# Second layer by single batches, expert rows added on TensorE, whole rows scattered to their experts

## The chip, the cores and the metric

The kernel runs on one core of one Trainium2 chip. The metric is the device time in microseconds (us) of one execution. TensorE is PE below, VectorE DVE, ScalarE ACT, GpSimd POOL, SyncE SP.

## What is computed

Two transformer layers over x, 8 batches of 128 rows of 256 numbers (1024 tokens). Each layer is cross-attention and then a mixture of experts. The change lies in the second layer, of which this is the reference:

```python
def _L1_xattn_ref(q, k, v):
    scale = 1.0 / jnp.sqrt(jnp.asarray(dk, dtype=q.dtype))
    scaled = jnp.einsum('bsd,bse->bde', q, k) * scale
    attn = jax.nn.softmax(scaled, axis=1)
    return jnp.einsum('bde,bse->bsd', attn, v)
...
def _L1_ffn_ref(x, router_w, expert_bias, gate_proj, up_proj, down_proj):   # 16 experts, 4 chosen, inner width 224
    logits = jnp.einsum('bsh,eh->bse', x, router_w) + expert_bias
    scores = jax.nn.softmax(logits, axis=-1)
    top_w, top_idx = jax.lax.top_k(scores, TOP_K)
    top_w = top_w / jnp.sum(top_w, axis=-1, keepdims=True)
    g = jnp.einsum('bsh,khe->bske', x, gate_proj)
    u = jnp.einsum('bsh,khe->bske', x, up_proj)
    out = jnp.einsum('bske,keh->bskh', jax.nn.silu(g) * u, down_proj)
    sel = jnp.take_along_axis(out, top_idx[..., None], axis=2)
    return jnp.sum(sel * top_w[..., None], axis=2)
...
x = x + _L0_xattn_ref(...)
x = x + _L0_ffn_ref(_layernorm(x), ...)          # 64 experts, 8 chosen
x = x + _L1_xattn_ref(_layernorm(x), ctx, ctx)
x = x + _L1_ffn_ref(_layernorm(x), ...)
```

## The kernel before

The program is a row of phases with a barrier of all engines between them. The first layer (projection, attention, experts) ends at about 449 us. The second layer is three phases.

**Features phase** (`features_phase`). SP loads, for each batch, the eight weighted expert rows of every token from the first layer (`ft_g_rows`, 1 MB a batch). The batches go in three groups, (0, 1), (2, 3, 4), (5, 6, 7). For a group DVE adds the eight rows and x (`Combine.dve_sum`), takes mean and variance, computes the inverse root with three Newton steps for the whole group (`Norm`), and writes the normalised rows. PE makes the scores (two matmuls of 128 by 256 a batch), DVE their maximum, ACT the exponentials and the scaled values, PE the sum over values (`ft_ps_out`, two matmuls of the same shape), DVE adds it to x. Then DVE normalises again (`Routing.dve_normalise`), PE turns the rows and multiplies by the gate. DVE's choice of the four experts (`dve_choose`) and the places in the lists (`dve_places`) of a group stand in the step of the next group. SP stores the normalised rows to `normed`; POOL scatters one number for each choice into a table, 32 indirect transfers in all. `Plan` turns the counts into a list of tiles, and then SP loads the weights of the first six tiles.

**Tiles phase** (`tiles_phase`). 42 tiles of at most 128 choices of one expert, in rounds of six buffers. For each tile POOL copies its column of the list (L1616), gathers the 128 rows from `normed` by an indirect transfer (L1620), and later scatters the result of the tile six before (L1625). PE turns the rows of the next tile, does the down matmuls of the tile two before, then the up matmuls of this one. SP loads a tile's weights, 448 and 224 KB, when the tile six before is through its down matmuls. The list has places for 128 choices in each tile; places that no choice fills gather some row and scatter it to spare rows.

**Last phase** (`last_phase`). SP loads four rows a token, DVE adds them with their weights to x, two batches interleaved, four operations each (L2045), ACT stores.

The first layer already routes one batch at a time with `RowRouting` and `Rstd`, and already scatters whole rows to their experts and clears the rows beyond. The order in all phases is written out by hand: each engine's block is a loop that issues in program order, and an instruction that waits holds all behind it on its engine or queue.

## Time and profile before

| | us |
|---|---|
| median of 3 runs (lowest, highest) | 775.46 (774.98, 780.38) |
| profiled execution, its own time | 776.06 |
| its span on the core | 774.3 |
| features phase, first rows there to the plan's end | 463.6 to 572.9 |
| tiles phase, first issue to last POOL issue | 593.2 to 742.7 |
| last phase to the span's end | 752.4 to 774.3 |

Share of the span busy: PE 62%, DVE 49%, POOL 44%, ACT 27%. The page gives the stages away by its clock row: the granted clock of TensorE is near full speed in the tiles and near half in the features phase. Times below are from the start of the span. The span and the execution's own time differ by 1.8 us, which lie around the span.

### The profile page before, as it was taken

To read this page: it belongs to the slowest core of one execution; us is meant where nothing else is said; L and a number is where in the kernel's file an instruction comes from. 1 tells how busy PE (TensorE), PEld (TensorE's weight loads), DVE (VectorE), ACT (ScalarE), POOL (GpSimd) and SP (SyncE) were. 2 spreads that over 40 slices of the span, in tenths; PEclk is the share of its full clock that TensorE was granted. 3 is DMA by queue.
4 is the path that set the end of the run, shared out by engine and by line. 5 is a ranking of instruction groups with operands and counts; after the bars stand their busy time and mean duration, and the time that the engine had idled before them with its cause. 6 is when DMAs were issued, how large, how long until landed. Compare 5 with 4: busy or idle time off the path is not lost. (4 is left out here: it accounts for less than half of the span.)

```text
span 774.3 us, 11100 instructions
## 1 busy us (share of the span) xinstructions
PE 477.6 (62%) x3303; PEld 360.8 (47%) x3303; DVE 380.1 (49%) x1226; ACT 207.7 (27%) x533; POOL 340.2 (44%) x464
## 2 busy tenths in 40 slices
PE   1715976887784209987899703254500889899920
PEld 1611533444442108876688602233400888888810
DVE  8955555888854503533344405878640123222217
ACT  0540453555563104322233201021100222222200
POOL 9483210555554533644455510030552566666510
PEclk9965897999977558999999955565655799999965
DMA  5199896764889638899954239100034499999716
GB/s 164 54 197 302 319 294 178 200 168 138 264 287 348 235 119 261 273 331 302 305 183 158 78 115 402 62 1 21 21 88 136 128 294 291 287 294 291 235 46 252
DMA packets 83086, 157.18 MB, mean 203 GB/s; under 512 B 12523, under 2 KB 53493, under 8 KB 81248
## 3 DMA queue, kind: packets, MB, share of 16 engines
q1 hardware_dynamic: 54928, 91.89, 37.7%
q10 hardware_dynamic: 14944, 32.71, 13.5%
q0 software_dynamic: 13168, 32.02, 12.4%
q8 instruction: 22, 0.36, 0.2%
q14 instruction: 24, 0.20, 0.1%
HBM read 102.95 MB, written 56.12 MB: 205 GB/s over the span
## 5 line engine op out<-in xcount | busy, mean ns | idle before, releaser
L1140 DVE TENSOR_REDUCE at_top<-at_ps_top 128x2 f32<-128x512 f32 x128 | 83.5, 685 | 50.7 <-PE at_ps_top L1051 49.7
L1514 POOL DMA_INDIRECT rows<-hd_out,hd_rows x64 | 62.2, 972 | 68.6 <-DVE hd_out L1465 45.9
L1367 PE MATMUL hd_ps_up<-hd_x_turned,e_arena 128*128 128x160 f32 x512 | 84.8, 310 | 0.0
L1213 ACT ACTIVATE at_prob<-at_ps_score 128x512 f32<-128x512 f32 x128 | 71.6, 593 | 44.8 <-PE at_ps_score L1069 44.3
L1672 PE MATMUL l_ps_up<-l_x_turned,e_up_w 128*112 128x128 f32 x672 | 82.8, 278 | 0.0
L1672 PEld LDWEIGHTS l_ps_up<-l_x_turned,e_up_w 128*112 128x112 f32 x672 | 81.6, 182 | 2.6
L1367 PEld LDWEIGHTS hd_ps_up<-hd_x_turned,e_arena 128*128 128x128 f32 x512 | 78.2, 197 | 8.9 <-issue 6.2
L845 POOL DMA_INDIRECT held<-e_extended,e_address x64 | 62.8, 980 | 34.3 <-issue 18.9
L642 POOL DMA_INDIRECT table<-choice,ft_r_address x32 | 30.6, 957 | 104.4 <-DVE ft_r_address L633 95.6
L1051 PE MATMUL at_ps_top<-e_arena 96*128 96x256 bf16 x256 | 57.0, 312 | 26.4 <-PEq L110 21.7
L1502 DVE TENSOR_TENSOR hd_inner<-hd_silu,hd_ps_up 128x160 f32<-128x160 f32 x64 | 20.5, 321 | 77.9 <-ACT hd_silu L1452 77.9
L1069 PE MATMUL at_ps_score<-e_arena 99*128 99x256 bf16 x256 | 52.1, 294 | 8.7 <-DMA e_arena<-at_top_rows 8.7
L1761 DVE TENSOR_TENSOR l_inner<-l_silu,l_ps_up 112x256 f32<-112x256 f32 x42 | 17.7, 421 | 79.6 <-ACT l_silu L1711 79.6
L1620 POOL DMA_INDIRECT l_rows<-normed,l_column x42 | 41.0, 976 | 33.1 <-POOL l_column L1616 33.1
L1625 POOL DMA_INDIRECT rows<-l_out,l_target x42 | 41.3, 983 | 18.2 <-issue 9.8
L1081 PE MATMUL at_ps_out<-at_prob,e_arena 128*32 128x256 f32 x512 | 44.5, 423 | 4.0 <-ACT at_out L1196 3.6
L1943 PE MATMUL ft_ps_scores<-ft_x_norm,ft_keys 128*128 128x256 f32 x32 | 14.6, 645 | 51.0 <-DVE ft_x_norm L161 51.0
L1051 PEld LDWEIGHTS at_ps_top<-e_arena 96*128 96x128 bf16 x256 | 23.8, 106 | 43.7 <-issue 23.6
L1654 PE MATMUL l_ps_out<-e_down_w,l_inner 112*128 112x256 f32 x168 | 43.3, 380 | 0.1
L1662 PE MATMUL l_ps_x<-identity,l_rows 128*128 128x128 f32 x84 | 18.1, 298 | 40.8 <-DMA l_rows<-normed,l_column 40.7
L1452 ACT ACTIVATE hd_silu<-hd_ps_up 128x160 f32<-128x160 f32 x64 | 19.5, 304 | 85.3 <-PE hd_ps_up L1367 85.3
L1465 DVE TENSOR_SCALAR hd_out<-hd_ps_out,hd_rows 128x256 f32<-128x256 f32 x64 | 31.0, 484 | 21.2 <-PE hd_ps_out L1373 19.4
(277 smaller groups left out, 867.3 us busy)
## 6 DMA issues: line engine op xcount, KB each, us to landing
e_up_w<-in_up SPq DMA_DIRECT2D x42, 448.0 KB, 4.5
held<-e_empty ACTq DMA_DIRECT2D x16, 960.0 KB, 6.9
e_arena<-in_weights ACTq DMA_DIRECT2D x32, 384.0 KB, 5.1
e_arena<-in_weights SPq DMA_DIRECT2D x32, 384.0 KB, 11.7
hd_rows<-held SPq DMA_DIRECT2D x15, 768.0 KB, 10.8
e_down_w<-in_down SPq DMA_DIRECT2D x42, 224.0 KB, 5.6
ft_g_rows<-rows SPq DMA_DIRECT2D x8, 1024.0 KB, 10.9
parts<-op_parts SPq DMA_DIRECT2D x8, 576.0 KB, 6.5
```

Source lines behind the costliest of these rows:

```text
L845: self.nc.gpsimd.indirect_dma_start(self.held_dram, to, self.held.extended[:, b, :], None).then_inc(self.held.scattered, 16)
L1051: last = nc.tensor.matmul(ps_top[at % TOPS][:, half, :], q_in[n][0:TOP, columns(at, half)], k_in[n][0:TOP, columns(at)], start=True, stop= ...
L1069: last = nc.tensor.matmul(ps_score[at % SCORES][:, half, :], k_in[n][0:ROWS, columns(at, half)], q_in[n][0:ROWS, columns(at)], start=True, ...
L1081: last = nc.tensor.matmul(ps_out[32 * j:32 * j + VW, g % 2, :], v_in[:, b, half, 4 * g + j, :], prob[(4 * group + j) % RING][:, half, :], ...
L1140: nc.vector.reduce_max(top[:, 2 * h:2 * h + 2], ps_top[at % TOPS][:], AX_X).then_inc(top_found, 1)
L1213: nc.scalar.activation(prob[at % RING][:], ps_score[at % SCORES][:], ACT.Exp, scale=scale).then_inc(prob_ready, 1)
L1367: op = nc.tensor.matmul(ps_up[e % 2][:, part, :], w[:, k, part * P:(part + 1) * P], x_turned[g % 2][:, j, k, :], start=k == 0, stop=k == 1)
L1514: nc.gpsimd.indirect_dma_start(rows_out, to, out_ap, None, bounds_check=TOKENS * LAYER0.chosen - 1, oob_is_err=False).then_inc(semaphore, 16)
L1620: nc.gpsimd.indirect_dma_start(rows[u][:], None, normed_dram, of).then_inc(gathered[u], 16)
L1625: nc.gpsimd.indirect_dma_start(rows_out, to, out[u][:], None).then_inc(stored[u], 16)
L1654: op = nc.tensor.matmul(ps_out[u % 2][:], inner[u % 2][:, c * P:(c + 1) * P], down_w[u][:, c, :], start=c == 0, stop=c == C - 1)
L1672: op = nc.tensor.matmul(ps_up[u % 2][:, part, c * P:(c + 1) * P], up_w[u][:, k, at:at + W], x_turned[u % 2][:, k, :], start=k == 0, stop=k ...
```

## The change

The second layer takes the first layer's scheme.

- Features by single batches, steps t = 0 to 9. DVE adds only the upper four expert rows to the lower four (`halve`). PE adds those four and x through the identity in one accumulation, `ps_x`, and the attention's sum goes into the same accumulation. The first inverse root moves to POOL (`pool_scale`: a power and two Newton steps), ACT applies both normalisations and copies x back to SBUF.
- Routing by `RowRouting`: the row, with the weights and targets of all experts behind it (288 numbers), is scattered to `listed`, which has 1024 places for each expert; 32 indirect transfers as before, of 1152 bytes a row. No `normed`, no table.
- Tiles: POOL clears the places of a tile that no row fills (an indirect transfer that leaves out the filled ones), SP waits for that and loads the tile as a plain block, then its weights. DVE picks the weight and the target by the expert's number and weights the result. Targets of empty places are out of bounds and are left out.
- Last phase: DVE adds by halves and to x, batch by batch.

```diff
 class Rstd:
+    def pool_scale(self, pool, link, b):
+        pool.wait_ge(self.known, b + 1)
+        link(nc.gpsimd.tensor_scalar(full, self.mean_var[:, 1:2], EPS, None, ALU.add))
+        link(nc.gpsimd.tensor_tensor(root, full, self.power[:], ALU.pow))
+        for _ in range(NEWTON - 1):
+            link(nc.gpsimd.tensor_tensor(square, root, root, ALU.mult))
+            link(nc.gpsimd.tensor_scalar(work, square, full, -0.5, ALU.mult, ALU.mult))
+            link(nc.gpsimd.tensor_scalar(root, work, 1.5, root, ALU.add, ALU.mult))
+        nc.gpsimd.tensor_scalar(shift, self.mean_var[:, 0:1], root, -1.0, ALU.mult, ALU.mult).then_inc(self.ready, 1)
...
 def features_phase
         @block.gpsimd
+            for t in STEPS:
+                if t < B:
+                    first.pool_scale(pool, link, t)
+                if t >= 2:
+                    for k in range(layer.chosen):
+                        routing.pool_scatter(pool, t - 2, k)
         @block.tensor
+            def add_rows(b):
+                pe.wait_ge(halved, b + 1)
+                if b >= 2:
+                    pe.wait_ge(x_kept, b - 1)
+                    pe.wait_ge(routing.normed, b - 1)
+                for k in range(HALF):
+                    nc.tensor.matmul(ps_x[b % 2][:], consts.identity[:], rows[b][:, k, :], start=k == 0, stop=False)
+                nc.tensor.matmul(ps_x[b % 2][:], consts.identity[:], x_all[:, b, :], start=False, stop=True).then_inc(summed, 1)
...
         @block.vector
+            routing.dve_start(link)
+            halve(0)
+            for t in STEPS:
+                if t < B:
+                    dve.wait_ge(summed, t + 1)
+                    first.dve_stats(dve, link, t, ps_x[t % 2][:])
+                if 1 <= t <= B:
+                    dve.wait_ge(attended, t)
+                    second.dve_stats(dve, link, t - 1, ps_x[(t - 1) % 2][:])
+                    second.dve_scale(dve, link, t - 1)
+                if t >= 2:
+                    routing.dve_targets(dve, link, t - 2)
+                    routing.dve_places(dve, link, t - 2)
+                if t < B:
+                    dve.wait_ge(scored, t + 1)
+                    link(nc.vector.reduce_max(top[:], ps_scores[t % 2][:], AX_X))
+                    nc.vector.tensor_scalar(minus_top[t % 2][:], top[:], -scale, None, ALU.mult).then_inc(top_known, 1)
+                if t + 1 < B:
+                    halve(t + 1)
+                if 1 <= t <= B:
+                    routing.dve_choose(dve, link, t - 1)
+                if t < B:
+                    dve.wait_ge(expo_ready, t + 1)
+                    nc.vector.reciprocal(share[t % 2][:], total[t % 2][:]).then_inc(share_ready, 1)
+                if t == B:
+                    plan.dve_plan(dve, link)
...
 def tiles_phase
         @block.sync
+            def load_rows(i, u):
+                c = sp.value_load(experts.tile_column[0:1, bass.ds(i * U + u, 1)], min_val=0, max_val=layer.columns)
+                sp.wait_ge(cleared[u], i * 16 + 16)
+                sp.dma_start(rows[u][:], by_tile[bass.ds(c, 1)].rearrange("a p n -> (a p) n")).then_inc(rows_loaded[u], 16)
...
                     sp.wait_ge(down_done, i * U + u - U + 1)
+                    load_rows(i, u)
                     experts.load(sp, i, u)
         @block.gpsimd
             with pool.Fori(1, last + 1) as i:
                 for u in range(U):
                     pool.wait_ge(out_kept, i * U + u - U + 1)
-                    gather(i, u)
+                    clear(i, u)
                     scatter(i - 1, u)
         @block.vector
+            def pick(i, u, free):
+                e = dve.value_load(experts.tile_expert[0:1, bass.ds(i * U + u, 1)], min_val=0, max_val=E - 1)
+                nc.vector.tensor_copy(weight[u][:], rows[u][:, bass.ds(e * 2 + D, 1)])
+                nc.vector.tensor_copy(target[u][:], rows[u].bitcast(I32)[:, bass.ds(e * 2 + (D + 1), 1)])
```

The order on PE in the features phase, around the second group, before (`ft_ps_out` is the attention's sum, `ft_r_ps_narrow` holds logits and ranks, an x4 or x6 is two matmuls for each batch of the group):

```order
L533 MATMUL ft_r_ps_turned<-identity,ft_r_norm 128x128 x4
L548 MATMUL ft_r_ps_narrow<-ft_gate,ft_r_turned_sb 128x16 x4
L1943 MATMUL ft_ps_scores<-ft_x_norm,ft_keys 128x256 x6
L613 MATMUL ft_r_ps_narrow<-l_mask,earlier 128x16 x2
L615 MATMUL ft_r_ps_narrow<-l_mask,ones 128x16
L1952 MATMUL ft_ps_out<-ft_expo,ft_vals_shared 128x256 x6
```

The same place now, step 2 (turn of batch 1, scores of batch 2, logits of batch 1, the adding of batch 3, rank of batch 1, attention's sum of batch 2):

```order
L593 MATMUL ft_ps_turned<-identity,e_extended 128x128 x2
L1728 MATMUL ft_ps_scores<-ft_x_norm,ft_keys 128x256 x2
L604 MATMUL ft_ps_logits<-ft_gate,ft_r_turned_sb 128x16 x2
L1718 MATMUL ft_ps_x<-ft_rows,identity 128x256 x4
L1719 MATMUL ft_ps_x<-x_all,identity 128x256
L637 MATMUL ft_ps_rank<-bases,ones 128x16
L639 MATMUL ft_ps_rank<-e_mask,ones 128x16
L641 MATMUL ft_ps_rank<-e_mask,earlier 128x16
L1734 MATMUL ft_ps_x<-ft_expo,ft_vals_shared 128x256 x2
```

Five matmuls of 128 by 256 now stand ahead of the attention's sum in each step, and the turn of one batch stands ahead of the scores of the next.

SP's queue in the tile loop, one tile, before:

```order
L447 TENSOR_LOAD l_tile_expert
L447 ISA x2
L449 ISA
L449 DMA e_up_w<-in_up 128x896
L449 ISA
L449 DMA e_down_w<-in_down 112x512
```

And now (`listed` is the DRAM table of whole rows; the wait for the clearing is ahead of L1429):

```order
L1427 TENSOR_LOAD e_tile_column
L1427 ISA x2
L1429 ISA
L1429 DMA l_rows<-listed 128x288
L413 REGISTER_ALU
L413 TENSOR_LOAD e_tile_expert
L413 ISA x2
L415 ISA
L415 DMA e_up_w<-in_up 128x896
L415 ISA
L415 DMA e_down_w<-in_down 112x512
```

The load of the rows came from POOL's queue to SP's, ahead of the same tile's weights and behind those of the tile before.

## Rows read from the trace of the kernel before

**Rows 1.** Windows by stage: length, busy PE, PEld, DVE, ACT, POOL; clock, DMA, GB/s.

```profile
463.60:572.90 109.30, 42.84 (x158) 31.66 (x158) 80.08 (x374) 16.84 (x59) 22.23 (x24) 0.56 0.25 93
...
600.70:742.70 142.00, 127.29 (x924) 117.09 (x924) 38.09 (x126) 31.61 (x85) 88.33 (x123) 0.97 0.81 251
```

**Rows 2.** Timeline, POOL in the tiles: start, length, engine, line, operation, [idle before].

```profile
651.62 0.20 POOL L1616 COPY l_column<-l_lists 128x2 int32 x1
652.60 0.97 POOL L1620 DMA_INDIRECT l_rows<-normed,l_column  x1 [0.79 <-POOL l_column L1616]
653.87 0.99 POOL L1625 DMA_INDIRECT rows<-l_out,l_target  x1 [0.30 <-issue]
...
655.85 0.99 POOL L1620 DMA_INDIRECT l_rows<-normed,l_column  x1 [0.79 <-POOL l_column L1616]
```

**Rows 3.** Timeline, DVE's copy of a result ahead of the first of these.

```profile
649.89 0.41 DVE L1755 COPY l_out<-l_ps_out 128x256 f32<-128x256 f32 x1
```

**Rows 4.** One tile's answer (l_rows): landing of its transfers from issue.

```profile
DMA to landing us min/median/max: 2.7/5.0/6.2
```

**Rows 5.** Timeline, end of the features phase and the first issue of the tiles.

```profile
572.61 0.28 DVE L1843 CAST l_tile_expert<-ft_r_ps_turned 1x128 int32<-1x128 f32 x1
...
582.78 0.33 SPq L449 DMA_DIRECT2D e_down_w<-in_down  x1
582.78 0.96 POOL L642 DMA_INDIRECT table<-choice,ft_r_address  x1 [0.31 <-issue]
593.22 0.33 SPq L1598 DMA_DIRECT2D l_choices<-table  x1
```

**Rows 6.** Timeline, PE in the features phase: two batches, then three.

```profile
473.80 3.75 PE L1943 MATMUL ft_ps_scores<-ft_x_norm,ft_keys 128*128 128x256 f32 x8 [32.62 <-DVE ft_x_norm L161]
...
535.18 5.49 PE L1943 MATMUL ft_ps_scores<-ft_x_norm,ft_keys 128*128 128x256 f32 x12 [8.78 <-DVE ft_x_norm L161]
```

**Rows 7.** Groups by form, DVE in the features phase.

```profile
L1875 DVE TENSOR_TENSOR ft_g_rows<-ft_g_rows 128x1024 f32<-128x1024 f32 x8 | 9.8, 1221 | 5.2 <-DMA ft_g_rows<-rows 5.2
...
L1995 DVE TENSOR_REDUCE ft_top<-ft_ps_scores 128x2 f32<-128x512 f32 x8 | 5.5, 692 | 7.7 <-PE ft_ps_scores L1943 7.7
L1875 DVE TENSOR_TENSOR ft_g_rows<-ft_g_rows 128x512 f32<-128x512 f32 x8 | 5.5, 692 | 0.3
...
L1875 DVE TENSOR_TENSOR ft_g_rows<-ft_g_rows 128x256 f32<-128x256 f32 x8 | 3.4, 425 | 0.3
```

**Rows 8.** Timeline, first layer, one batch: statistics, root, ACT, turn, mask.

```profile
244.63 0.43 DVE L729 BATCH_NORM_STATS2 at_n_stats<-x_all 128x6 f32<-128x256 f32 x1
...
247.28 0.60 ACT L772 ACTIVATE e_extended<-x_all,at_n_scale 128x256 f32<-128x256 f32 x1 [7.38 <-DVE at_n_scale L743]
...
247.94 0.69 PE L778 MATMUL at_ps_merge<-identity,e_extended 128*128 128x128 f32 x2 [3.87 <-ACT e_extended L772]
...
251.16 0.20 DVE L801 TENSOR_SCALAR e_mask<-at_r_taken 128x64 bf16<-128x64 f32 x1
```

**Rows 9.** Timeline, a chain of seven dependent small POOL operations, first and last.

```profile
88.01 0.25 POOL L1022 TENSOR_SCALAR at_top_cut<-at_top 128x16 bf16<-128x16 f32 x1 [9.24 <-DVE at_top L1140]
...
89.83 0.25 POOL L1028 TENSOR_SCALAR at_top_parts<-at_top_rest 128x16 f32<-128x16 f32 x1
```

**Rows 10.** Windows around a busy stretch of PE in the features phase.

```profile
501.40:506.20 4.80, 4.75 (x11) 3.86 (x12) 2.84 (x9) 1.25 (x6) 0.00 (x0) 0.50 0.00 0
506.30:509.90 3.60, 0.67 (x5) 0.14 (x3) 2.76 (x20) 1.94 (x8) 0.00 (x0) 0.96 0.00 0
```

**Rows 11.** DMA issues by line in the tiles: KB each, median landing.

```profile
e_down_w<-in_down SPq DMA_DIRECT2D x34, 224.0 KB, 5.7
rows<-l_out,l_target POOLq DMA_INDIRECT x39, 5.4
```

**Rows 12.** Timeline, last phase, one pair of batches on DVE.

```profile
757.36 0.88 DVE L2045 SCALAR_TENSOR_TENSOR ls_x_sum<-ls_rows,l_weight,x_all 128x256 f32<-128x256 f32 x2 [16.45 <-DMA ls_rows<-rows]
758.28 2.71 DVE L2045 SCALAR_TENSOR_TENSOR ls_x_sum<-ls_rows,l_weight,ls_x_sum 128x256 f32<-128x256 f32 x6
```

803 lines of the change are left out of this document (293 added, 510 removed).

## The prediction, made before the changed kernel had run

> **What bounds the kernel now.** I read the page first, then windows by stage. The second layer's features phase takes 109.3 us with the granted clock at 0.56 on average and DVE busy 80.08 of them; the tiles take 142 us with PE busy 127.3 at a clock of 0.97 [rows 1]. In the features phase the reader is to see an engine chain: the work of a group goes DVE, PE, DVE, ACT, PE, DVE, and PE does 42.8 us of work in it.
>
> In the tiles PE looks like the bound, but POOL sets the pace. One gather starts at 652.60, the next at 655.85: 3.25 us a tile, of which two indirect transfers are 0.97 + 0.99, with 0.79 and 0.30 ahead of them, and the copy of the column 0.2 [rows 2]. POOL never pauses there. PE's own work is 127.3 / 42 = 3.03 us a tile. DVE has the result of a tile copied at 649.89 + 0.41 = 650.30 [rows 3], and POOL comes to it, with the copy of the column, at 651.62 [rows 2]: it is 1.3 us late. A gather lands 5.0 us after its issue in the middle of them, 2.7 at the least [rows 4].
>
> At the end of the features phase the plan is ready at 572.9, POOL ends its last scatter at 583.74 and SP its last weight load at 583.1; the tiles begin at 593.22 [rows 5].
>
> **The change part by part.**
>
> *The round of a batch.* The features phase becomes eight rounds, each closed by a dependence: the sum of batch t on PE, the second normalisation and turn of it, then PE's scores of batch t+1 (they stand behind the turn), DVE's maximum, DVE's halving for batch t+2 (behind the maximum), PE's adding for t+2, then the sum of batch t+1 behind it. I price one round at the low clock. A matmul of 128 by 256 is two records of about 0.43: the twelve records of three batches take 5.49 and the eight of two take 3.75, so four more cost 1.74 [rows 6].
>
> - attention's sum on PE, same shape as the scores: 1.71; hand-over to DVE 0.4
> - second statistics and root on DVE: statistics begin at 244.63, the root's chain ends at 247.28 in the first layer: 2.65 [rows 8]
> - ACT's normalisation 0.60 and PE's turn 0.69 [rows 8]
> - scores 1.71, hand-over 0.37
> - maximum 0.69 [rows 7], its scaling and the waits 0.2
> - halving, 128 by 1024: 1.22 [rows 7]
> - five adding matmuls, ten records: 4.27
> - rank 0.35 (estimate, some matmuls of 16 columns), further hand-overs 0.3
>
> Sum 15.2 us. With all PE work at half its length (0.5 instead of 1, for 8.7 us of it) it would be 10.8. Which clock? After 4.8 us of dense work at 0.50 the clock stood at 0.96 for the next 3.6 us and fell back once PE had been nearly idle [rows 10]. In a round PE is dense from the adding to the end of the sum, 6.3 us, and idle for the 3.6 us of the second normalisation. So I expect the high clock for the last part of each round only, and take 14.5.
>
> *The sum of the features phase.* Rows of batch 0 are there at 463.6. Halving 1.2, adding 4.3 + 0.4, statistics 0.65, POOL's root 2.9, ACT 0.6, scores 2.1, maximum 0.9, halving 1.2, adding of batch 1 4.3, sum 1.7: the first sum ends at about 484. Six rounds of 14.5 give 571. The last round has no halving and adding, which are 5.5, but then the other arm (exponentials, choice of the batch before, shares) is 1.6 longer: 11.3, so 582. Then normalising, turning and choosing as in the first layer, 244.63 to 251.36, 6.7 us [rows 8], count 0.8, and a plan of about twenty small DVE operations of 0.2, 4.2: ready at 594 with hand-overs. Before it was 572.9: **+21 us**. What this removes (half the DVE adding, one of the normalising writes) lies off the new round or is paid back: DVE adds eight rows to one in 1.22 + 0.69 + 0.43 + 0.43 now [rows 7]; the change keeps 1.22 and puts 4.27 on PE at the low clock.
>
> *POOL's root* I cost at nothing. It is nine dependent small operations; seven such start 0.30 apart, 88.01 to 89.83 [rows 9], so 2.7 plus what the power costs more, which no row shows. Its cover: the adding ends 2.1 before the sum of the batch before, so statistics are known 1.0 before it, and ACT needs the result when the second root is ready, 3.0 after it, less its own 0.6: 3.4 us. Each us beyond is a us in each of eight rounds. Lower bound 0, upper bound 2 us a round (the power as dear as a 128 by 512 operation, far off). The Trainium skill, "GPSIMD Engine Reference", section "Engine selection", sends elementwise work with two inputs to VectorE, since GPSIMD is about two times slower on it; the rows have 0.30 against about 0.20 a step, and by the page's ratio the chain would be 3.6 us, 0.2 beyond the cover.
>
> *The end of the phase.* POOL no longer waits for its scatters to land before the barrier. SP's loads now end it, 10.2 after the plan; before, the landing of POOL's last scatter did, 582.78 + 2.7 as the least gather [rows 4] = 585.5, against 583.1. **−2.4 us** [rows 5]. The scatters of a batch, four of 1.27, fit in a round.
>
> *The tiles.* POOL has the same two indirect transfers and one copy a tile, so its 3.25 us stay; a clearing may have nothing to write, but it must still be issued. What grows is the way from a tile's end to the rows of the tile six later: gather (5.0) becomes clearing, SP's issue 0.4, and a load behind the weights of the tile before on SP's queue. DVE's pick, with its read of the expert's number ahead of the product, holds the copy of the result by some 0.5 more. PE turns a tile one step ahead and brings it down two steps later, so three of six steps of the loop are PE's; an added us is spread over the other three. The slack is POOL's lateness of 1.3 and three steps of 3.25 − 3.03 = 0.22 on PE: 2.0, and I take 1.9. Clearing: between the gather's 2.7 and 5.0 [rows 4]; it queues behind the scatter issued 1.97 before it, which lands in 5.4 [rows 11], so 3.4 at this pace, and I take 3.0 for a queue less full. Load: 2.7 at the least, at the most 5.7 as the weights [rows 11]; I take 3.5, nearer the gather, since it is 147 KB and not 224. Added: 3.0 + 0.4 + 3.5 + 0.5 − 5.0 = 2.4; (2.4 − 1.9) / 3 = 0.17 a tile, and with unevenness I take 0.22 for 41 tiles: **+9 us**. Ends: 2.7 + 0.4 + 2.7 + 0.5 − 5.0 = 1.3, within the slack, so 0, and (5.0 + 0.4 + 5.7 + 0.5 − 5.0 − 1.9) / 3 = 1.6 a tile, +64, which can't hold, since at a slower pace the DMA engines are less full (share 0.81 over the phase [rows 1]); I cut it at +30.
>
> *The last phase.* A pair of batches takes 0.88 + 2.71 = 3.6 [rows 12], four pairs 14.4. Now a batch is 0.69 + 0.43 + 0.43 [rows 7] and 0.1: 13.2, and it starts after one load, not two: **−1.9**. The first layer is the same work.
>
> Sum against the profiled execution: 776.06 + 21 − 2.4 + 9 − 1.9 = 801.8. The median of the runs lies 0.6 below that execution: 801.
>
> **The rivals.**
>
> 1. *Tiles keep POOL's pace* (+0 to +3), features as forecast: 776.06 + 21 − 2.4 + 1.5 − 1.9 − 0.6 = 794. For it: POOL is late now, so transfers have slack. Against: two transfers in a row where one stood. Chance 0.19.
> 2. *The clock stays high in the rounds*, which ends on the other side. A round of 10.8, first sum at 478 and last round 9.2 give a plan at 564.5 instead of 572.9: −8. With the tiles at POOL's pace: 776.06 − 8 − 2.4 + 0 − 1.9 − 0.6 = 763; with the +9, 772. It decides at a round of about 13 without tile loss. For it: one dense stretch did raise the clock [rows 10] and PE's share in a round rises to 60%. Against: 3.6 us without PE work in each round. Chance 0.11.
> 3. *The rows wait for the weights.* SP's queue serves in order, and the load of the rows lands with the weights of the tile before, at 5.7: added 3.4 + 0.4 + 5.7 + 0.5 − 5.0 = 5.0, (5.0 − 1.9) / 3 = 1.0 a tile, of which 0.6 is left, since a slower pace empties the queue: 41 × 0.6 = +25, total 817. For it: the weights' 5.7 against the pace of 3.25 [rows 11]. Against: each load is issued a whole tile after the weights ahead. The Trainium skill, "DMA: Bandwidth & Descriptors", sections "Queues, rings and completion order" and "SWDGE vs HWDGE vs iDMA", has this rule: one queue's descriptors are consumed in order on each DMA engine, while queues of POOL and SP are served in turn. By that rule the gather shared with the weights and the new load stands behind them. Chance 0.12.
> 4. *POOL's root is late*, by 1 to 2 us a round: +8 to +16, total 809 to 817. Chance 0.08, on top of 3 or alone.
>
> **How the numbers follow.** The forecast, 795 to 812, has 0.47; the rest, 0.03, is a gain that I don't see. The predicted time is the forecast's, 801. The range reaches down into rival 2 and up over rival 3: 777 to 824. This kernel's runs tell about 1% from no change, 767.7 to 783.2. Faster: half of rival 2 and a little, 0.08. Same: the other half and the low ends, 0.12. Slower: 0.80.
>
> **What would show it.** Features: five adding matmuls in 4.3 us or near 2.2; the start of one `ft_ps_scores` to the next 14 to 15 us apart; the plan's last operation near 594; DVE's root done while ACT is not waiting for POOL. Tiles: start to start of clearings 3.25 (rival 1) or 3.4 to 3.5 (forecast) or 3.8 and more (rival 3); PE's busy share in the tiles below today's 127.3 of 142. Last phase near 20 us. I am wrong if the granted clock in the features phase is above 0.8, or if clearing and load together land within 5 us.

## The result, and the profile after

| | kernel before | changed kernel |
|---|---|---|
| median, us | 775.2 (774.7 to 780.4, 4 runs) | 807.8 (806.3 to 809.3, 4 runs) |
| profiled execution's own time, us | 776.06 | 807.32 |
| its span, us | 774.3 | 805.6 |

The ratio is 1.039 (95% interval 1.035 to 1.043): slower, as forecast, 6.8 us above the predicted 801 and within the range. The spans differ by 31.3 us. Where they lie:

| stage | before, us | after, us | difference | forecast |
|---|---|---|---|---|
| first layer, to DVE's first addition in the features phase | 463.60 | 466.82 | +3.2 | 0 |
| features, from there to the plan's last operation | 109.3 | 123.7 | +14.4 | +21 |
| plan's end to the first turn of a tile | 27.8 | 22.1 | −5.8 | −2.4 |
| tiles, first turn to the end of POOL's last scatter | 142.0 | 164.8 | +22.8 | +9 |
| last scatter to the end | 31.6 | 28.2 | −3.4 | −1.9 |

So the total came out near the forecast partly by luck: two errors of opposite sign, −6.6 and +13.8, partly cancelled. The experiments go to these two terms.

The windows of the two stages, in the columns of [rows 1] (length, busy PE, PEld, DVE, ACT, POOL, clock, DMA share, GB/s). The features phase, then the tiles from the first turn to the last:

```profile
466.80:590.60 123.80, 67.83 (x246) 51.51 (x246) 57.66 (x272) 32.92 (x104) 50.90 (x100) 0.65 0.28 108
```

```profile
612.62:764.77 152.15, 122.56 (x875) 110.81 (x875) 41.56 (x158) 31.77 (x82) 83.12 (x117) 0.97 0.78 237
```

In the features phase DVE's load fell from 80 to 58 us and PE's rose from 43 to 68, and the phase is longer: a chain and not an engine's load sets it. In the tiles PE is busy for 0.81 of the time; before it was 0.90 in the stretch of [rows 1], which runs on to the last scatter, and 0.91 (119.80 of 132.13 us) to the last turn, with the same work at the same clock of 0.97.

One round of the features phase, timeline of PE, DVE, ACT and POOL, the lines that carry it (columns as in [rows 2]):

```profile
504.10 1.92 PE L1728 MATMUL ft_ps_scores<-ft_x_norm,ft_keys 128*128 128x256 f32 x4
506.05 0.69 DVE L1807 TENSOR_REDUCE ft_top<-ft_ps_scores 128x2 f32<-128x512 f32 x1 [2.98 <-PE ft_ps_scores L1728]
506.86 1.22 DVE L1790 TENSOR_TENSOR ft_rows<-ft_rows 128x1024 f32<-128x1024 f32 x1
508.13 3.78 PE L1718 MATMUL ft_ps_x<-ft_rows,identity 128*128 128x256 f32 x8 [1.45 <-DVE ft_rows L1790]
511.70 0.70 PE L1719 MATMUL ft_ps_x<-x_all,identity 128*128 128x256 f32 x2
512.31 1.11 PE L1734 MATMUL ft_ps_x<-ft_expo,ft_vals_shared 128*128 128x256 f32 x4
513.46 0.43 DVE L515 BATCH_NORM_STATS2 ft_n_stats<-ft_ps_x 128x6 f32<-128x256 f32 x1 [0.38 <-PE ft_ps_x L1734]
515.96 0.16 DVE L530 SCALAR_TENSOR_TENSOR ft_n_scale<-ft_n_mean_var,ft_n_scale 128x1 f32<-128x1 f32 x1
516.20 0.29 POOL L546 TENSOR_SCALAR ft_n_scale<-ft_n_mean_var,ft_n_scale 128x1 f32<-128x1 f32 x1
516.53 0.56 ACT L550 ACTIVATE ft_x_norm<-ft_ps_x,ft_n_scale 128x256 f32<-128x256 f32 x1 [6.31 <-POOL ft_n_scale L546]
516.99 0.56 ACT L550 ACTIVATE e_extended<-ft_ps_x,ft_n_scale 128x256 f32<-128x256 f32 x1
517.60 0.69 PE L593 MATMUL ft_ps_turned<-identity,e_extended 128*128 128x128 f32 x2 [4.17 <-ACT e_extended L550]
```

This is the forecast's chain link by link: scores, maximum, halving, adding, sum, second root, normalisation, turn. The starts of `ft_ps_scores` are at 476.8, 490.6, 504.1, 518.1, 531.7, 545.2, 558.9 and 572.4, so 13.7 us apart on average. Three things are to be seen that the forecast did not have. The sum takes 1.11 and not 1.71, at a granted clock of 1.00 (windows, 512.30 to 513.50). ACT waits for POOL's root until 516.49, 0.4 us after DVE's root; and as it normalises the next batch first (`ft_x_norm`), the normalisation that the turn needs (`e_extended`) starts at 516.99, 0.87 us after DVE's root. And DVE stands idle for 2.98 us just before the maximum, with the halving, on which PE waits 1.45 us, queued behind it.

The way of one tile's rows in the tile loop, timeline, from the turn of the tile three earlier to the turn of this one:

```profile
640.18 0.44 PE L1495 MATMUL l_ps_x<-identity,l_rows 128*128 128x128 f32 x2 [0.62 <-DMA l_rows<-listed]
641.52 0.48 DVE L1564 TENSOR_SCALAR l_out<-l_ps_out,l_weight 128x256 f32<-128x256 f32 x1
641.64 0.97 POOL L1459 DMA_INDIRECT rows<-l_out,l_target  x1 [0.30 <-issue]
642.96 0.18 POOL L1450 COPY l_index<-e_clear_rows 128x1 int32 x1 [0.35 <-issue]
644.03 0.98 POOL L1454 DMA_INDIRECT listed<-l_empty,l_index  x1 [0.89 <-POOL l_index L1450]
647.72 0.34 SPq L1429 DMA_DIRECT2D l_rows<-listed  x1
651.88 0.33 PE L1495 MATMUL l_ps_x<-identity,l_rows 128*128 128x128 f32 x1 [1.06 <-DMA l_rows<-listed]
```

I took these steps for all tiles from the ninth on, from the timelines of both kernels; the means, in us, of 34 tiles:

| | turn of tile n−3 to the result of tile n−6 | result to POOL's transfer for tile n | transfer to SP's issue | to the turn of tile n | sum |
|---|---|---|---|---|---|
| before | 1.43 | 2.96 (gather) | | 5.42 | 9.81 |
| after | 1.50 | 2.64 (clearing) | 3.95 | 3.22 | 11.31 |

The sum is three periods, where a period is the time from one tile's turn to the next: 3.27 us a tile before, 3.77 after. Over the last 34 turns that is 17.2 us; the first turns have 2.9 more and the way from the last turn to the last scatter 2.6 more, together the 22.7.

The landing of transfers in the middle of the tiles, in the columns of [rows 11]:

```profile
e_down_w<-in_down SPq DMA_DIRECT2D x32, 224.0 KB, 4.8
l_rows<-listed SPq DMA_DIRECT2D x34, 144.0 KB, 2.8
listed<-l_empty,l_index POOLq DMA_INDIRECT x34, 3.3
```

### The profile page after: what moved, and what is told of

Read it like the earlier page. It is cut to its first block and busy times, and to the rows that moved or that the text cites. A ratio compares the mean times of both kernels' runs of the same rounds, so it can differ in the third digit from the quotient of the medians.

```text
span 805.6 us, 12068 instructions
## 1 busy us (share of the span) xinstructions
PE 506.9 (63%) x3391; PEld 382.6 (47%) x3391; DVE 362.2 (45%) x1161; ACT 223.9 (28%) x578; POOL 364.1 (45%) x538
## 3 DMA queue, kind: packets, MB, share of 16 engines
q0 software_dynamic: 13680, 31.41, 10.8%
## 5 line engine op out<-in xcount | busy, mean ns | idle before, releaser
L1559 DVE COPY l_weight<-l_rows 128x1 f32 x42 | 6.5, 154 | 127.9 <-ACT l_silu L1540 105.5
L900 PE MATMUL at_ps_score<-e_arena 99*128 99x256 bf16 x256 | 53.8, 302 | 9.5 <-DMA e_arena<-at_top_rows 9.4
L1454 POOL DMA_INDIRECT listed<-l_empty,l_index x42 | 41.3, 982 | 37.4 <-POOL l_index L1450 37.4
L1718 PE MATMUL ft_ps_x<-ft_rows,identity 128*128 128x256 f32 x64 | 29.7, 645 | 34.8 <-DVE ft_rows L1790 34.8
L674 POOL DMA_INDIRECT listed<-e_extended,e_address x32 | 34.3, 1071 | 34.5 <-ACT e_extended L657 24.6
L1540 ACT ACTIVATE l_silu<-l_ps_up 112x256 f32<-112x256 f32 x42 | 16.1, 383 | 94.0 <-PE l_ps_up L1505 94.0
## 6 DMA issues: line engine op xcount, KB each, us to landing
hd_rows<-held SPq DMA_DIRECT2D x15, 768.0 KB, 10.3
```

The lines of the kernel that those rows point to most:

```text
L674: self.nc.gpsimd.indirect_dma_start(self.held_dram, to, self.held.extended[:, b, :], None).then_inc(self.held.scattered, 16)
L900: last = nc.tensor.matmul(ps_score[at % SCORES][:, half, :], k_in[n][0:ROWS, columns(at, half)], q_in[n][0:ROWS, columns(at)], start=True, ...
L1454: nc.gpsimd.indirect_dma_start(listed_dram, to, empty[:], None, bounds_check=E * TOKENS + P - 1, oob_is_err=False).then_inc(cleared[u], 16)
```

## Experiments on the features phase

Each row below gives the profiled execution's stages, cut as in the table above. Totals are medians; the kernel before had medians of 778.6 to 781.1 on the same chips as these runs, so stages tell more than totals. Each stage is from one profile. Where the code of a stage is the same, profiles differ: the features phase of the changed kernel, e2, e6, e8 and e11 takes 123.7 to 125.9, the tiles of the changed kernel, e1, e3 and e4 164.1 to 168.0. A difference of that size is not read as an effect.

| kernel | total | rounds | features | tiles |
|---|---|---|---|---|
| changed | 807.8 | 13.7 | 123.7 | 164.8 |
| e1_halve_first | 797.7 | 11.7 | 111.5 | 164.1 |
| e3_tree_on_dve | 801.2 | 13.1 | 118.9 | 168.0 |
| e4_root_on_dve | 812.7 | 14.8 | 130.4 | 165.6 |
| e2_clear_ahead | 786.3 | 13.7 | 124.3 | 144.9 |
| e8_index_ahead | 795.0 | 13.9 | 125.2 | 154.6 |
| e11_rows_on_act | 811.1 | 13.9 | 125.9 | 171.0 |
| e6_no_weights | 789.3 | 13.7 | 123.8 | 146.8 |
| e5_add_ahead | 762.0 | 9.7 | 101.7 | 143.9 |
| e10_scatter_between | 760.5 | 9.7 | 101.5 | 139.3 |

**The order on DVE: e1_halve_first.**

```diff
+                if t + 1 < B:
+                    halve(t + 1)
                 if t < B:
                     dve.wait_ge(scored, t + 1)
                     link(nc.vector.reduce_max(top[:], ps_scores[t % 2][:], AX_X))
                     nc.vector.tensor_scalar(minus_top[t % 2][:], top[:], -scale, None, ALU.mult).then_inc(top_known, 1)
-                if t + 1 < B:
-                    halve(t + 1)
```

> Only DVE's order in a round changes: the halving for the next batch stands ahead of the wait for the scores, where DVE is idle for 2.98 us in the changed kernel, and not behind the maximum. If the round is set by the adding on PE (it starts at 508.13, 1.45 us after PE's last operation ahead of it, and ends at 512.4, when the shared values have been there since 510.2), seven rounds of eight lose 1.4 us each: starts of ft_ps_scores 12.2 to 12.4 us apart, features phase 123.8 down to 114, total near 798. Rival: the other branch (maximum, exponentials, choice, shares, values) or the halving itself holds the round, and it loses less than 0.5 us: total 804 to 808.

Measured: starts of `ft_ps_scores` 11.4 to 12.1 apart, the phase 12.3 us shorter, total 797.7 (ratio to the kernel before 1.027, 1.019 to 1.035). The work is the same; a round lost the 1.45 us and some 0.5 more, and the high clock comes earlier in the round: over the adding of the round below the granted clock is 0.69 on average, over that of the changed kernel's round above 0.55. In the timeline of e1 the halving lies beside the normalisation, and the adding follows without a wait and takes 3.00 for its eight records, where it took 3.78:

```profile
499.25 1.22 DVE L1790 TENSOR_TENSOR ft_rows<-ft_rows 128x1024 f32<-128x1024 f32 x1
502.09 3.00 PE L1718 MATMUL ft_ps_x<-ft_rows,identity 128*128 128x256 f32 x8
505.44 1.11 PE L1734 MATMUL ft_ps_x<-ft_expo,ft_vals_shared 128*128 128x256 f32 x4
```

So 12.3 of the 14.4 us that the features phase lost are had back by moving the halving, with PE's share of the adding as it is.

**The adding itself: e3_tree_on_dve.**

```diff
-                for k in range(HALF):
-                    nc.tensor.matmul(ps_x[b % 2][:], consts.identity[:], rows[b][:, k, :], start=k == 0, stop=False)
+                nc.tensor.matmul(ps_x[b % 2][:], consts.identity[:], rows[b][:, 0, :], start=True, stop=False)
...
-                nc.vector.tensor_tensor(rows[b][:, 0:HALF, :], rows[b][:, 0:HALF, :], rows[b][:, HALF:, :], ALU.add).then_inc(halved, 1)
+                link(nc.vector.tensor_tensor(rows[b][:, 0:4, :], rows[b][:, 0:4, :], rows[b][:, 4:8, :], ALU.add))
+                link(nc.vector.tensor_tensor(rows[b][:, 0:2, :], rows[b][:, 0:2, :], rows[b][:, 2:4, :], ALU.add))
+                nc.vector.tensor_tensor(rows[b][:, 0, :], rows[b][:, 0, :], rows[b][:, 1, :], ALU.add).then_inc(halved, 1)
```

> DVE adds the eight rows to one (1.22 + 0.69 + 0.43), PE only adds that row and the token's own: two matmuls of 128 by 256 where there were five, six records of 0.43 less. DVE's two further additions, 1.1 us, stand in the same place on the path. If the adding on PE at the low clock makes the round long, a round loses 2.6 - 1.1 = 1.5 us: starts of ft_ps_scores 12.2 apart, total 797. Rival: with less dense work PE is not given the high clock at the end of a round, attention's sum takes 1.7 and not 1.1, scores are never below 1.9, and the round loses 0.5 or less: total 803 to 808.

Measured: rounds 13.1, phase 4.8 us shorter, total 801.2, between the two expectations. By the rounds the rival is nearer: of the 1.5 us a round 0.6 is left, scores are never below 1.9 and the sum is at 1.7 or more in every round. The groups on PE in the window 476 to 575 show where the rest went, behind the first bar busy us and mean ns of one record. The changed kernel:

```profile
L1728 PE MATMUL ft_ps_scores<-ft_x_norm,ft_keys 128*128 128x256 f32 x32 | 13.2, 557 | 4.9 <-ACT ft_x_norm L550 4.9
L1734 PE MATMUL ft_ps_x<-ft_expo,ft_vals_shared 128*128 128x256 f32 x28 | 7.7, 397 | 0.0
```

and e3:

```profile
L1733 PE MATMUL ft_ps_x<-ft_expo,ft_vals_shared 128*128 128x256 f32 x32 | 15.8, 648 | 0.7 <-ACT ft_vals_shared L1780 0.7
L1727 PE MATMUL ft_ps_scores<-ft_x_norm,ft_keys 128*128 128x256 f32 x32 | 15.4, 637 | 4.9 <-ACT ft_x_norm L550 4.9
```

The same matmuls of the sum take 648 ns a record where they took 397, and those of the scores 637 instead of 557; the granted clock from the first to the last start of the scores is 0.57 instead of 0.68. Here, what is taken away from PE lets the clock fall for the work behind it.

**POOL's root: e4_root_on_dve.**

```diff
                 if t < B:
                     dve.wait_ge(summed, t + 1)
                     first.dve_stats(dve, link, t, ps_x[t % 2][:])
+                    first.dve_scale(dve, link, t)
```

with POOL's `pool_scale` left out.

> The root of the first normalisation is worked out by DVE, right behind its statistics, and not by POOL. By my theory POOL's place is worth its price: DVE's root takes 2.1 us, of which 0.5 would have been a wait for the sum, so the second statistics begin 1.6 us later, less 0.4 that ACT now waits for POOL: +1.2 us in each of eight rounds, rounds 14.8 apart, total 816 to 820. Rival (POOL's root is what holds the round): ACT goes on earlier, rounds 13.2 or less, total 804 or less.

Measured: rounds 14.2 to 15.1, mean 14.8, phase 6.7 us longer, total 812.7. Rival 4 in the strong form, POOL's root as the thing that holds the round, is refuted; the total stays below the expected 816. It does not say that POOL's root is free. In the changed kernel the normalisation ahead of the turn starts 0.8 to 1.0 us after DVE's root in each of the first seven rounds, since ACT waits for POOL first; in e4 it starts 0.03 to 0.04 after it. This remains of rival 4. e4 takes it away and the round is still 1.1 us longer, as DVE's two roots then stand one behind the other.

**The adding in PE's idle time: e5_add_ahead.** With the earlier clearing of e2 (next section) kept, PE adds batch t+2 behind the sum of batch t, with a third buffer in PSUM:

```diff
-        ps_x = [s.psum(f"ps_x{n}", [P, D]) for n in range(2)]
+        ps_x = [s.psum(f"ps_x{n}", [P, D]) for n in range(3)]
...
-                if t + 1 < B:
-                    add_rows(t + 1)
                 if 1 <= t <= B:
                     routing.pe_rank(pe, t - 1)
                 if t < B:
                     attend(t)
+                if t + 2 < B:
+                    add_rows(t + 2)
...
-                    first.pool_scale(pool, link, t)
+                    first.pool_scale(pool, link, t + 1)
...
+                if t + 2 < B:
+                    halve(t + 2)
+                if t + 1 < B:
+                    first_stats(t + 1)
                 if t < B:
                     dve.wait_ge(scored, t + 1)
```

> With the earlier clearing of e2 kept, PE adds the rows two batches ahead, right behind a batch's attention sum, where it is idle for 4.2 us in the changed kernel while DVE works out the second root; a third buffer in PSUM makes that possible, and DVE's halving stands ahead of the maximum. If a round is the chain root - normalisation - turn - scores - maximum - exponentials - shared values - sum, of 10.6 us by the changed kernel's rows (2.66 + 1.1 + 0.7 + 1.9 + 0.9 + 1.05 + 0.9 + 1.4), starts of ft_ps_scores stand 10.0 to 10.8 apart, the features phase falls from 124 to 100 to 104 us, total 763 to 768, below the kernel before. Rival: the adding (4.3 us at the low clock) does not fit into the idle time and holds up the turn, or the halving holds up the maximum: rounds of 11.5 or more as in e1, total 773 to 776.

Measured: 762.0 us, 0.9775 of the kernel before (0.971 to 0.984), starts of `ft_ps_scores` 8.7 to 10.2 apart, 9.7 on average and so a little shorter than expected, features 101.7, where the kernel before needs 109.3. The lines of a round, timeline of e5:

```profile
524.52 2.08 PE L1743 MATMUL ft_ps_x<-ft_expo,ft_vals_shared 128*128 128x256 f32 x4 [0.75 <-ACT ft_vals_shared L1791]
526.39 2.50 PE L1727 MATMUL ft_ps_x<-ft_rows,identity 128*128 128x256 f32 x8
528.73 0.59 PE L1728 MATMUL ft_ps_x<-x_all,identity 128*128 128x256 f32 x2
529.92 0.44 PE L593 MATMUL ft_ps_turned<-identity,e_extended 128*128 128x128 f32 x2 [0.60 <-ACT e_extended L550]
530.19 1.03 PE L1737 MATMUL ft_ps_scores<-ft_x_norm,ft_keys 128*128 128x256 f32 x4
```

The adding is done 0.6 us before the turn can start, so PE's adding has left the chain. The high clock has moved with it: the turn (0.44, it was 0.69 in the round above) and the scores (1.03, they were 1.92) run at a granted clock of 1.00 here and in all rounds but the last ones, while the sum, now ahead of the adding, is at 0.50 in this round and takes 2.08 where it took 1.11. The granted clock from the second to the last start of scores is 0.84. And since POOL works out its root a batch ahead, the normalisation of this round starts 0.04 us after DVE's root, where it was 0.87. The run makes these changes together and does not part them. A round is 2.0 us shorter than in e1.

## Experiments on the tiles

**Clearing one group earlier: e2_clear_ahead.**

```diff
             for u in range(U):
                 clear(0, u)
-            with pool.Fori(1, last + 1) as i:
+            for u in range(U):
+                pool.wait_ge(cleared[u], 16)
+                pool.sem_inc(parted, 1)
+                clear(1, u)
+            with pool.Fori(1, last) as i:
                 for u in range(U):
+                    pool.wait_ge(cleared[u], i * 16 + 16)
+                    pool.sem_inc(parted, 1)
+                    clear(i + 1, u)
                     pool.wait_ge(out_kept, i * U + u - U + 1)
                     pool.sem_inc(parted, 1)
-                    pool.wait_ge(cleared[u], i * 16)
-                    pool.sem_inc(parted, 1)
-                    clear(i, u)
                     scatter(i - 1, u)
+            for u in range(U):
+                pool.wait_ge(out_kept, last * U + u - U + 1)
+                pool.sem_inc(parted, 1)
+                scatter(last - 1, u)
```

> Each tile's rows in the expert's list are cleared one group (six tiles) earlier, and the clearing no longer waits for a result; nothing is left out. My reading of the changed kernel: a tile's turn to the turn three later takes 11.3 us, of which clearing with SP's start is 3.95 and POOL's copy and register reads 2.6. If that chain sets the pace, POOL's own 3.35 us a tile sets it now, and the tiles lose 0.34 x 36 and a little at the end, 13 us: total 794 to 796. Rival (the rows wait behind the weights in SP's queue): from the issue of the rows to the turn grows or stays, the pace stays at 3.6 or more, total 804 to 808. If POOL's two transfers and the copy are not 3.35 but more when they stand together, 800.

Measured: 786.3 us (1.012 of the kernel before, 1.004 to 1.019), tiles 144.9 instead of 164.8, period 3.36 us over the last 34 turns. POOL's own pace sets it. That the tiles lost 20 us and not 13 comes mostly from the start and the end of the loop, which I had left out: the first seven turns took 4.3 us less and the way from the last turn to the end of the last scatter 1.5. The other 14 are the period, which fell by 0.41 and not by 0.34. The same transfers run, clearing included, so the loss of the tiles lies in the clearing's place in the chain. By this run rival 1, the tiles at POOL's pace, is what the change gives when the clearing does not wait for a result.

**What fills the 7.2 us from clearing to turn: e6_no_weights and e11_rows_on_act.**

```diff
                     load_rows(i, u)
-                    experts.load(sp, i, u)
...
-                pe.wait_ge(weights_loaded[u], (i + 1) * (16 * len(experts.transfers)))
+                pe.wait_ge(weights_loaded[u], 16 * len(experts.transfers))
```

> The changed kernel, but only the first six tiles' weights are loaded, and every later tile is computed with those; all else is issued as before. If the rows wait behind the weights in SP's queue, or for the DMA engines, then from the issue of the rows to the turn (3.2 us) it takes 2.3 or less, from clearing to SP's issue (3.95) 3.2 or less, and the tiles run at POOL's 3.35 us, total near 795. If these 7.2 us are the transfers' own latency, they stay above 6.6 together and the pace above 3.5, total 802 to 806.

This kernel leaves out the weights of all tiles from the seventh on, so only its times are of use. Measured: 789.3 in one run, tiles 146.8, period 3.34. The landing of transfers in the same window as above, e6:

```profile
l_rows<-listed SPq DMA_DIRECT2D x37, 144.0 KB, 2.1
rows<-l_out,l_target POOLq DMA_INDIRECT x38, 2.4
listed<-l_empty,l_index POOLq DMA_INDIRECT x36, 2.1
```

Rows land in 2.1 instead of 2.8 and the clearing in 2.1 instead of 3.3: the weights cost the two transfers 1.9 us together, which is more than the 1.3 us by which three periods exceed POOL's pace (11.3 against 3 x 3.34). The steps agree with the first of the two expectations: from clearing to SP's issue 2.38 instead of 3.95, from there to the turn 2.20 instead of 3.22, means of the same 34 tiles. Of the 2.6 us together the landings are 1.9; the rest lies around them, and no run here says where. Which part of the 0.7 for the rows is SP's queue, e11 tells; ACT waits for the clearing and issues the load, behind its copy of the turned rows:

```diff
                     sp.wait_ge(down_done, i * U + u - U + 1)
                     sp.sem_inc(sp_parted, 1)
-                    load_rows(i, u)
                     experts.load(sp, i, u)
...
+            def load_rows(i, u):
+                act.wait_ge(down_done, i * U + u - U + 1)
+                c = act.value_load(experts.tile_column[0:1, bass.ds(i * U + u, 1)], min_val=0, max_val=layer.columns)
+                act.wait_ge(cleared[u], i * 16 + 16)
+                act.dma_start(rows[u][:], by_tile[bass.ds(c, 1)].rearrange("a p n -> (a p) n")).then_inc(rows_loaded[u], 16)
```

> The changed kernel, with the load of a tile's rows issued by ACT on its own DMA queue and not by SP, where the weights are; ACT does it 0.3 us later than SP would. The landing of the rows, median 2.8 us with the weights and 2.1 without them, tells what costs the 0.7: in the order of one queue it falls to 2.3 or less, and the tiles lose 0.1 us each or more, total 800 to 805; if all queues share the DMA engines it stays at 2.7 or more, total 806 to 812.

Measured: 811.1 (two runs), tiles 171.0. Landing in the same window:

```profile
l_rows<-listed ACTq DMA_DIRECT2D x30, 144.0 KB, 2.5
```

2.5 lies between both expectations; from issue to turn it takes 2.53 instead of 3.22 (2.20 without the weights), so about half of what the weights add to the rows, or somewhat more, is the queue that they share. The time went the other way: from clearing to issue it takes 5.22 instead of 3.95, of which the clearing's own landing is 0.1 (3.4 for 3.3), so ACT comes to the load later than SP by more than 1 us and not by the 0.3 that I had taken from the turn's place. Of the 6.2 us that the tiles are longer, 4.7 are in the first seven turns. So the total is in the range of the second expectation for another reason than its own. The Trainium skill, "DMA: Bandwidth & Descriptors", section "Queues, rings and completion order", has descriptors of one queue consumed in order; the landings of e11 agree with it in direction, but what the order costs the rows here is 0.3 us by the landings and 0.7 by the way from issue to turn, not the weights' 4.8.

**POOL's way from a result to its transfer: e8_index_ahead.**

```diff
-                    pool.wait_ge(out_kept, i * U + u - U + 1)
-                    pool.sem_inc(parted, 1)
                     pool.wait_ge(cleared[u], i * 16)
                     pool.sem_inc(parted, 1)
                     clear(i, u)
+                    pool.wait_ge(out_kept, i * U + u - U + 1)
+                    pool.sem_inc(parted, 1)
+                    send_clear(u)
                     scatter(i - 1, u)
```

where `clear` now only copies the index, and `send_clear` issues the clearing.

> The changed kernel, with POOL's reads of registers and its copy of the index ahead of the wait for the result; only the clearing itself and the scatter stand behind it. From DVE's result to the clearing it takes 2.64 us in the changed kernel: 0.48 of the result, 1.0 of waits and reads, 1.07 of the copy. If that is latency, it falls to 0.8 to 1.0, the chain to 9.6 us for three tiles, and POOL's own 3.35 sets the pace: 20 us less in the tiles' phase or a little under, total 790 to 794. If POOL comes late because it is busy with the scatter ahead, it stays above 2 us and the total above 803.

Measured: 795.0 in two runs (1.021, 1.015 to 1.027). From result to clearing it takes 1.66 instead of 2.64 us, three periods 10.8 instead of 11.3, tiles 10 us shorter. So the reads and the copy, 1.0 of the 2.64 us, stood in the chain for no need. The rest, 0.48 for the result and some 1.2 from its end to the clearing, stays: more than the 0.8 to 1.0 expected, and the pace is 3.6, not POOL's 3.35.

**The slack of the kernel before: e7_before_held_up and e9_before_copies.** Both hold up each tile's result in the kernel before, and nothing of the change is in them.

```diff
                     nc.vector.tensor_copy(target[u][:], column[u][:, 0, 1:2])
+                    nc.vector.tensor_tensor(held_up[:, u % 3], held_up[:, 3], held_up[:, 3], ALU.add)
                 nc.vector.tensor_copy(out[u][:], ps_out[u % 2][:]).then_inc(out_kept, 1)
```

> The kernel before, and nothing of the change: DVE does an addition of 128 by 1024 that nobody needs (1.22 us) ahead of the copy of each tile's result, so that POOL gets it later. The forecast gave the way from a result to the next rows a slack of 1.9 us: then nothing changes, 775. By the two traces POOL's way from the copy of the result to its transfer fell only from 2.96 to 2.64 when it was pressed, so the slack is 0.3: then (1.22 - 0.32) / 3 = 0.3 us a tile, for 36 tiles +11, total 786 to 788.

Measured: 799.3, tiles 161.0, period 3.75. That is more than either theory has, and it is no test of the slack: POOL's own work grew. POOL in the tiles, e7:

```profile
L1626 POOL DMA_INDIRECT rows<-l_out,l_target x33 | 38.4, 1163 | 10.1 <-issue 10.1
L1621 POOL DMA_INDIRECT l_rows<-normed,l_column x32 | 32.3, 1010 | 25.1 <-POOL l_column L1617 25.1
L1617 POOL COPY l_column<-l_lists 128x2 int32 x32 | 15.5, 486 | 0.2
```

and the same lines of the kernel before:

```profile
L1625 POOL DMA_INDIRECT rows<-l_out,l_target x38 | 37.4, 983 | 15.7 <-issue 9.2 <-DVE l_out L1755 6.5
L1620 POOL DMA_INDIRECT l_rows<-normed,l_column x34 | 33.2, 978 | 26.7 <-POOL l_column L1616 26.7
L1616 POOL COPY l_column<-l_lists 128x2 int32 x33 | 6.5, 198 | 0.1
```

With the waits of 0.30 and 0.79 that makes 1.16 + 1.01 + 0.49 + 1.09 = 3.75 us a tile. DVE's addition of 128 by 1024 in SBUF lengthens what POOL does meanwhile. So I held the result up by three copies out of PSUM:

```diff
+                    for k in range(3):
+                        nc.vector.tensor_copy(held_up[:, u, k, :], ps_out[u % 2][:])
```

> The kernel before again, with the result of a tile held up by three more copies of it out of PSUM (0.41 us each, into tiles that nobody reads) instead of the addition of 128 by 1024, which stretched POOL's instructions (its copy from 0.20 to 0.49 us, the scatter from 0.98 to 1.16) and so made POOL's own pace 3.75 us. If POOL's instructions keep their length now and the slack is 0.3 us, the pace is (9.81 + 1.2 - 0.3) / 3 = 3.57, tiles' phase +11, total 786 to 789. With a slack of 1.9 nothing changes, 776 to 779. If copies out of PSUM stretch POOL's instructions too, its busy time in the tiles exceeds 90 us and nothing is learned of the slack.

Measured: 788.3 in two runs (1.011 of the kernel before, 1.003 to 1.019), tiles 149.2, 7.2 us longer and not 11 or nothing, and POOL's instructions keep their length (987, 977 and 190 ns). The result comes 0.99 us later, not 1.2; from result to gather it takes 2.42 instead of 2.96; three periods are 10.26. The slack of the kernel before is therefore 2.96 − 2.42 = 0.54 us, and what exceeds it goes to the period by a third: (0.99 − 0.54) / 3 = 0.15. That the period grew by 0.15 is no second proof of this, since the way from gather to turn kept its 5.42 and the sum then has to come out. The slack of 1.9, by which nothing would have changed, is refuted; the slack of 0.3 is too small. The total of 788.3 lies in the range for 0.3 only because the kernel before had 781.1 on this chip and not 775.

**The scatter between copy and clearing: e10_scatter_between.** On top of e5:

```diff
                     clear(i + 1, u)
                     pool.wait_ge(out_kept, i * U + u - U + 1)
                     pool.sem_inc(parted, 1)
                     scatter(i - 1, u)
+                    send_clear(i + 1, u)
```

> e5 with POOL's scatter between the copy of the index and the clearing that uses it: the 0.89 us for which POOL waits between the two are covered by the scatter (0.30 + 0.97), so that POOL's own work on a tile falls from 3.35 to 2.8 us or less. PE's 3.03 a tile is then the bound: period 3.05 to 3.15, tiles' phase 10 us shorter, total 751 to 756. Rival: the DMA engines, busy for 0.89 of the time at 3.34 us a tile, can't carry more, period 3.25 or more, total 758 to 762.

Measured: 760.5, 0.976 of the kernel before (0.970 to 0.982); tiles 139.3 instead of 143.9, period 3.20. Both theories have a part: POOL is no longer the pace, but PE's 3.03 isn't reached. The window of the tiles and PE's wait in it, e10:

```profile
591.10:719.20 128.10, 119.03 (x874) 109.62 (x874) 39.68 (x155) 30.17 (x82) 82.53 (x116) 0.98 0.91 279
```

```profile
L1508 PE MATMUL l_ps_x<-identity,l_rows 128*128 128x128 f32 x76 | 15.9, 290 | 7.1 <-DMA l_rows<-listed 6.8
```

The DMA engines are busy for 0.91 of the time, and PE waits for rows again. Whether it is their throughput that ends it was not tried. Against e5 the total is 1.4 us lower, less than these runs can tell; the 4.6 us in the tiles are seen in one profile each.

## Why the prediction was right, and where its terms were off

*The round of a batch*: right as a chain, 0.8 us too long. Its links came as priced, the adding 4.27 from 508.13 to 512.40 against 4.27, statistics to root 2.66 against 2.65, scores 1.92 against 1.71 (1.1 to 1.2 in three of the eight). The sum at the end ran at the high clock, as argued from [rows 10], 1.11 for 1.71, and so, for the most part, did the scores in those three; against that ACT's wait for POOL added 0.8. The sum of the phase: to the end of the first attention sum 19.2 (forecast 20.4), six rounds 81.8 (87), the last 11.5 (11.3), to the plan's end 11.2 (12). That is 123.7 for 130.4. The forecast took 14.5 between its ends of 15.2 and 10.8, with no more to place it there than the guess of a high clock in the last part; 13.7 was right.

*What I had not asked* is why the halving stands behind the maximum. It was priced as a link (1.22) like any other, though DVE is idle before it. e1 shows that its place, with the clock that follows from it, is worth 12 us, and e5 that PE's adding too can leave the chain. Most of the loss in the features phase belongs to the order within the round.

*POOL's root at nothing*: this failed, by 0.8 us a round. The chain took 3.3 us (472.77 to 476.07 in the first round, 513.18 to 516.49 in the round above) where 2.7 and an unknown power were set against a cover of 3.4. The power is 0.57. The cover was not 3.4: in the round above the statistics are known at 513.08 and the second root at 516.12, 3.04 later, and less the 0.56 of ACT's normalisation that is 2.5. The forecast had the statistics known 1.0 us before the end of the sum; it is 0.34, since the sum behind the adding ran at the high clock. The chain and its start, 3.4 us from the statistics on, exceed that by 0.9, and the normalisation starts 0.87 us after the root; over seven rounds it is 6.1 us. By the ratio of two of the Trainium skill ("GPSIMD Engine Reference", section "Engine selection") the chain would be an estimated 3.6 us; the trace has 3.3.

*The end of the phase*: −5.8 for −2.4, the right sign and mechanism with too small a size. SP's loads end it, 10.3 after the plan, as said. From SP's last issue the tiles began 10.1 us later before and 5.1 later now, so what held the barrier was worth 5.0 and not 2.4. I had taken the least gather, 2.7, for the landing of POOL's last scatter, and no row shows how long that takes beside the loads of weights; that it was this landing is inferred and wasn't tried. The first tile's rows come 0.9 us sooner after the barrier.

*The tiles*: +22.8 for +9; the step that failed is the slack. The added way was sized well: 0.07 for the picks where I had 0.5, and 3.95 + 3.22 − 5.42 = 1.75 for clearing, SP and load where I had 1.9. The slack was set at 1.9: POOL's lateness of 1.3 and three steps of PE's 0.22. Neither is slack in full. Of the lateness 1.0 us stays when POOL is pressed: in e9 it is 2.42, less 0.41 for the result and 0.99 from the copy of the column to the gather, and in the changed kernel 2.64 − 0.48 − 1.07 = 1.09. And PE's 0.22 is a wait inside the chain, not a reserve of it. Measured, the slack is 0.54 (e9). In the forecast's formula, with the 0.22 by which the pressed way from result to transfer is longer in the changed kernel (2.64 against 2.42): (0.07 + 0.22 + 1.75 − 0.54) / 3 = 0.50 a tile, which is 3.77 − 3.27. These are the differences of the table's steps put in another order, so that they add up is no test; e2 and e8, which take the clearing and the copy out of the chain, are. At 34 tiles that is 17 us, and the start and the end of the loop, not in the forecast, have 5.5. The term's range, 0 to +30, holds the 22.8.

*Rival 1* (POOL's pace) did not happen, but is what e2 gives. *Rival 2*: the clock in the phase is 0.65, and e3 shows that the mechanism in it exists. *Rival 3*: the load of the rows lands in 2.8, not in 5.7; that the weights slow both transfers is right (e6), by 1.9 us together. *Rival 4*: it had 1 to 2 us a round and came near its low end, 0.8 to 1.0 in seven rounds and 6.1 in all, inside a round that was shorter than forecast for other reasons.

*The last phase*: −3.4 for −1.9. From the last scatter to DVE's first addition 13.1 instead of 14.6 us, and eight batches in 12.4 instead of 14.3. The forecast had 1.2 for the batches, which became 1.9, and 0.7 for one load in place of two, for which it showed no row and which became 1.5. From the first load to the end it is 18.8 us, near 20 as said.

*The first layer* ended 3.2 us later, which no term has. In e7 and e9, whose first layer is that of the kernel before, it ends at 466.4 and 466.9; in the nine runs with that of the changed kernel, at 462.6 to 468.0. So it varies by 5 us from profile to profile, and the 3.2 are not laid to the change. Without them the total would be near 805.

The signs named ahead: adding near 4.3, yes; rounds of 14 to 15, just below (13.5 to 14.0); plan's end near 594, 590.6; ACT not waiting for POOL, no; clearings apart by 3.69 on average (3.33 to 4.27), between forecast and rival 3; PE's share lower, yes; clock below 0.8, yes; clearing and load not within 5 us, yes (6.1).

## What to carry to other kernels

An engine that comes late to a result is not free by the time that it is late: take off the fixed latency behind a wait (here 1.0 us on POOL for waits and register reads together), and count as slack only what falls away when the engine is pressed. In a loop that closes over several tiles a wait inside the loop is no reserve either. When a change makes a chain of engines, ask of each link whether it must stand in the chain at all: here the halving moved ahead of a wait gave back 12 us, and with the adding and the clearing moved ahead too the changed kernel was 2.2% faster than the kernel before (1.6 to 2.9%).

## What the runs showed of the hardware

- DVE's addition of 128 by 1024 in SBUF (1.22 us) lengthens POOL's instructions beside it: in e7 a copy of 0.20 us took 0.49 on average and up to 1.28, an indirect transfer of 0.98 up to 1.88. In the features phase of the changed kernel a scatter beside the halving took 1.71. DVE's copies of 128 by 256 out of PSUM did not (e9).
- From the end of a result that POOL waits for to POOL's next instruction, with the read of a register between them, about 1.0 us goes by (e9, and 1.09 in the changed kernel), and from its copy of an index to the indirect transfer that uses it 0.79 to 0.90; with another transfer put between the two, the gaps are 0.16 and 0.30 (e10).
- Less work on PE can be slower work: with six records fewer a round the granted clock fell from 0.68 to 0.57, and the same records of the sum took 648 instead of 397 ns (e3). With the work moved into the idle time, the clock rose to 0.84 (e5); it rose for the turn and the scores, and the sum went from 1.11 to 2.08 us.
- A transfer of 144 KB issued by SP landed in 2.1 us without the weights (e6) and in 2.8 behind them (the changed kernel); issued by ACT, on another queue beside them, in 2.5 (e11). All are medians.
